# A gated block's first turn: the low halves of W2 move from GpSimd to VectorE, one behind each gate product

## What is computed

```python
x = x + jnp.tanh(g_xattn[0]) * _L0_xattn_ref(ctx_1024, _layernorm(x, axis=-1), ...)
x = x + jnp.tanh(g_ffn[0]) * _L0_ffn_ref(_layernorm(x, axis=-1), ...)

def _expert_ffn(x, w1, wg, w2):
    return jax.nn.silu(x @ w1) * (x @ wg) @ w2
# in _L0_ffn_ref:
output = _expert_ffn(x, Ws1, Wsg, Ws2)
for e in range(NUM_ROUTED):                       # 7 experts, the best 3 of each row count
    w_e = jnp.sum(topk_probas * (topk_idxs == e), axis=-1)
    output = output + _expert_ffn(x, W1[e], Wg[e], W2[e]) * w_e[..., None]
```

## Time and profile before

| | |
|---|---|
| median of 3 runs | 1408.97 us (1408.61 to 1411.01) |
| profiled execution | 1408.53 us, span 1406.7 us |
| TensorE matmul busy | 1362.3 us (97%) |
| VectorE busy | 964.6 us (69%) |
| ScalarE busy | 618.5 us (44%) |
| GpSimd busy | 413.5 us (29%) |
| chain that ended last | PE 82%, DVE 11%, issue 4%, ACT 2% |

### The profile page before, as it was taken

The page is one execution under the profiler, slowest core; times in us unless marked ns, Lnnn a source line. Parts: engine busy times, 40 slices in busy tenths (PEclk is TensorE's granted clock), DMA queues, the critical chain, the costliest instruction groups (busy, mean ns, idle before and its releaser), DMA issues.

```text
span 1406.7 us, 18118 instructions
## 1 busy us (share of the span) xinstructions
PE 1362.3 (97%) x6290; PEld 1065.3 (76%) x6290; DVE 964.6 (69%) x1107; ACT 618.5 (44%) x1007; POOL 413.5 (29%) x224
## 2 busy tenths in 40 slices
PE   9888799999999999999999999999999999999999
PEld 4454577777777877888888877888888888888887
DVE  6999856799999764689888765598888732112111
ACT  6887455766556225544543235534543222111111
POOL 0000044788889310123332120133332211111111
PEclk8999999999999999999999999999999999999999
DMA  6344336676667853654565653655665555555552
GB/s 219 108 155 157 135 122 233 253 266 240 227 231 270 284 181 125 199 165 156 187 202 194 256 193 112 205 158 164 196 202 182 200 189 194 194 193 179 179 179 89
DMA packets 90797, 266.38 MB, mean 189 GB/s; under 512 B 11472, under 2 KB 11600, under 8 KB 90336
## 3 DMA queue, kind: packets, MB, share of 16 engines
q1 hardware_dynamic: 85472, 258.39, 53.6%
q10 hardware_dynamic: 5248, 6.96, 1.4%
HBM read 207.39 MB, written 57.93 MB: 189 GB/s over the span
## 4 chain that ended last, share of the span: by engine, by line
PE 82%; DVE 11%; issue 4%; ACT 2%; DMA 0%; ACTq 0%; DVEq 0%; POOL 0%
PE ps_hg L474 24%; PE ps_h L474 21%; PE ps_y L474 16%; PE ps_y L633 8%; DVE st L1180 7%; PE ps_mid L552 6%; DVE y_rows L1186 1%; DVE st L1171 1%; PE ps_mid L522 1%; PE ps_mid L515 1%; PE ps_mid L518 1%; PE ps_mid L474 1%; ACT dA L836 1%; PE ps_h L544 0%; PE ps_y L497 0%
## 5 line engine op out<-in xcount | busy, mean ns | idle before, releaser
L1444 POOL TENSOR_TENSOR h_lo<-h_tmp,h_hi 128x512 fp32r<-128x512 f32 x128 | 256.9, 2007 | 743.9 <-ACT h_hi L913 700.7
L474 PE MATMUL ps_h<-x_hi,w_split 128*128 128x512 f32 x1024 | 345.9, 399 | 1.6 <-DVE x_lo L1239 1.4
L474 PE MATMUL ps_hg<-x_hi,wg_split 128*128 128x512 f32 x1024 | 345.0, 398 | 0.1
L1309 DVE TENSOR_TENSOR h_tmp<-h_tmp,ps_hg 128x512 f32<-128x512 f32 x128 | 88.0, 688 | 318.5 <-PE ps_hg L474 317.5
L1180 DVE TENSOR_TENSOR_SCAN st<-dA,st 128x1024 f32<-128x1024 f32 x128 | 305.8, 2398 | 0.0
L474 PE MATMUL ps_y<-w_split,h_hi 128*128 128x512 f32 x1024 | 258.1, 400 | 0.0
L913 ACT ACTIVATE h_hi<-h_tmp 128x512 fp32r<-128x512 f32 x128 | 80.6, 630 | 350.0 <-DVE h_tmp L1309 350.0
L474 PEld LDWEIGHTS ps_h<-x_hi,w_split 128*128 128x128 f32 x1024 | 192.3, 188 | 42.0 <-DVE x_lo L1239 1.7
L474 PEld LDWEIGHTS ps_hg<-x_hi,wg_split 128*128 128x128 f32 x1024 | 192.3, 188 | 39.8 <-issue 0.5
L474 PEld LDWEIGHTS ps_y<-w_split,h_hi 128*128 128x128 f32 x1024 | 190.3, 190 | 38.5
L907 ACT ACTIVATE h_tmp<-ps_h 128x512 f32<-128x512 f32 x128 | 76.2, 595 | 293.1 <-PE ps_h L474 293.1
(11 more groups left out here) (143 smaller groups left out, 1127.5 us busy)
## 6 DMA issues: line engine op xcount, KB each, us to landing
w_split<-split_scratch SPq DMA_DIRECT2D x192, 512.0 KB, 5.0
wg_split<-split_scratch SPq DMA_DIRECT2D x96, 512.0 KB, 4.2
split_scratch<-w_split SPq DMA_DIRECT2D x64, 512.0 KB, 3.7
b_all<-xd_scratch SPq DMA_DIRECT2D x64, 256.0 KB, 4.1
split_scratch<-wg_split SPq DMA_DIRECT2D x32, 512.0 KB, 3.0
w_raw<-in_W_dram SPq DMA_DIRECT2D x14, 1024.0 KB, 7.1
wg_raw<-in_Wg_dram SPq DMA_DIRECT2D x7, 1024.0 KB, 9.7
dA<-in_x_dram SPq DMA_DIRECT2D x4, 1024.0 KB, 7.8
```

The source lines that it names most:

```text
L474: mm = pe.matmul(out_, lhs[a], rhs[c], start=first and q == 0, stop=last and q == len(sides) - 1)
L1309: dve.tensor_tensor(h_tmp[j % 2][:], h_tmp[j % 2][:], ps_hg[:], ALU.mult).then_inc(h_made, 1)
L1444: pool.tensor_tensor(h_lo[:, j, :], h_tmp[j % 2][:], h_hi[:, j, :].bitcast(F32), ALU.subtract).then_inc(hl_ready, 1)
```

## The change

In steps 1 to 7 of the first turn VectorE makes the low half of tile j of W2 directly behind product j. GpSimd's row of four is gone. TensorE, ScalarE and SyncE keep their instructions and their order.

```diff
+            def down_low(step, j):
+
+                dve.wait_ge(w2h, T * step + j + 1)
+                dve.tensor_tensor(half(2, j, 1), w_raw[2][:, j], half(2, j, 0).bitcast(F32), ALU.subtract).then_inc(w2l, 1)
+
             def step_(step, e, between=lambda p: None):
+
+                splits = isinstance(step, int) and 0 < step < STEPS
...
                     dve.tensor_tensor(h_tmp[j % 2][:], h_tmp[j % 2][:], ps_hg[:], ALU.mult).then_inc(h_made, 1)
+                    if splits:
+                        down_low(step, j)
                     between(2 * j + 1)
...
-            def split_down(step, tiles=range(T)):
-                for j in tiles:
-                    pool.wait_ge(w2h, T * step + j + 1)
-                    pool.tensor_tensor(half(2, j, 1), w_raw[2][:, j], half(2, j, 0).bitcast(F32),
-                                       ALU.subtract).then_inc(w2l, 1)
...
-                if split:
-                    split_down(step + 1)
```

## The result

The changed kernel takes 1480.67 us (median of 4 runs, 1479.36 to 1481.9) against 1408.79 us for the kernel before on the same chip (4 runs, 1407.59 to 1411.01): a ratio of 1.0508 [1.0493, 1.0523], 71.9 us slower. The profiled execution took 1481.8 us, with a span of 1480.0 us against 1406.7. The prediction said 1471 us, range 1440 to 1495.

A forecast was written before the change was run, and what follows sets the result against it. TensorE and VectorE both nearly full in a 41.06 us step, stretches hanging on VectorE's order. Step 2 17.4, four periods 42.6, step 7 1.2, clock 1.5: 62.7 us on 1408.5 gives 1471 us, range 1440 to 1495.

The forecast's parts named there:

- the queue: SyncE's DMAs behind the late W2 flag: 13.0 us from first issue to the row's landing, bounds 11 and 15.
- the clock: TensorE slow after resting at g = 10 in the down phase: 0.3 us for each of five rests, 1.5 us.
- four periods: Between the five late rows of steps 2 to 6: 51.7 us each against 41.06, together 42.6 us more.
- step 7: No row to wait for, two subtractions ahead of the residual: 1.2 us.
- the forecast of 271.3: Step 2: raw W1 lands at 271.3, not 260.5, behind 6.8 MB taking 19.8 us; ScalarE wants it at 263.14.
- the working of step 2: Late raw W1, then the late row, put product 0 of step 3 at 323.9, not 306.54: 17.4 us later.
- the prediction's walk: One step summed stretch by stretch from row landing to row landing: 51.7 us, with 14.2 from landing to product 0.
- The subtractions: Four added on VectorE per step, 0.60 us each: 2.4 us a step if port waits stay as they are.
- rival 1: Row comes in time after all, only VectorE's 2.4 us a step count: 14 us, 1423 us; chance 0.10.
- rival 2: GpSimd off the shared port makes VectorE faster, a step gains 1.9 us: 9.5 us, 1399 us; chance 0.04.
- Rival 3: Raw loads late in every step, not step 2 alone, each of four periods 3 us longer: 1483 us; chance 0.10.
- where PE waits for nothing: Place of GpSimd's removed row, 7.74 us a step: gives back GpSimd's time and perhaps some of VectorE's through the port.

The follow-up runs named there:

- Experiments 1: Kernel before, late flag alone: each W2 store on SyncE also waits for its product, GpSimd's row kept, no VectorE subtraction; 1465.51 us, ratio 1.0394.
- experiment 4: Changed kernel with SyncE's DMAs interleaved: W2 store j ahead of tile j's up stores, row behind tile 1's, raw W2 last; 1417.82 us, ratio 1.0053.
- experiment 2: Kernel before, GpSimd's row and early flag kept, plus an unused VectorE subtraction behind each product of steps 1 to 7; 1427.75 us, ratio 1.0134.
- experiment 3: Changed kernel with the load of the row of slots 8 to 11 issued before the W2 stores in steps 2 to 6; 1458.84 us, ratio 1.0347.
- Experiments 7: Kernel before with GpSimd's four W2 subtractions replaced by one-column memsets raising the same flags, low halves left stale; 1405.24 us, ratio 0.9972.
- experiment 9: Changed kernel with all four VectorE subtractions ahead of product 0, SyncE's order as in the kernel before; 1404.72 us, ratio 0.997.
- experiment 8: Changed kernel with interleaved SyncE order and VectorE's subtractions in pairs ahead of products 0 and 2; 1412.69 us, ratio 1.0029.

## Why the prediction came out as it did

**The mechanism was right.** VectorE waits for a DMA once in each of steps 2 to 6, ahead of the row product of slot 8; TensorE waits behind it; ScalarE waits once for raw W1; later steps are untouched. Experiments 1 and 4 show that flag and queue are the cause: one makes the loss without VectorE's work, the other has VectorE's work without the loss. The sum was 62.7 us and 73.3 were measured on the profiled execution's span. The missing 10.6 us are two terms sized too small, the queue (8.5 us) and the clock (5.5), and two sized too large (0.7 us in each of four periods, 0.8 in step 7); the rest comes to 0.2 us. That the sum is no further off is in part luck, as the errors have opposite signs.

**The queue: 13.0 us, measured 14.4.** From the first DMA behind the flag to the row's landing the five steps took 13.45, 16.0, 14.4, 13.4 and 14.8 us. I had argued that 13.0 should do because the queue starts empty, where the one that it was copied from had three stores ahead. The rate was lower: 315 GB/s in the window above against 344. Over the four periods the mean is 14.65, so 1.65 us each, 6.6 us. In step 2 the same queue makes ScalarE's wait end at 274.34:

```profile
274.34 0.63 ACT L898 ACTIVATE w_split<-w_raw 128x512 fp32r<-128x512 f32 x1 [9.56 <-DMA w_raw<-in_W_dram]
```

That row is from ACT's timeline of the changed kernel; the forecast of 271.3 was 272.9 with the 1.6 us by which this execution was late already, so 1.4 us more. The first row landed another 0.5 us late.

**The clock: 1.5 us for all rests, measured 7.0.** Two rows of PE's timeline, changed kernel:

```profile
287.42 1.11 PE L552 MATMUL ps_mid<-ident,st 128*128 128x128 f32 x4 [10.43 <-DVE st L1180]
...
318.23 1.09 PE L552 MATMUL ps_mid<-ident,st 128*128 128x128 f32 x4 [7.15 <-DVE y_rows L1186]
```

Four transposes take 1.1 us here and 0.66 at full clock. In step 2 TensorE rested from 277.0 to 287.4; the granted clock was 0.50 (1.2 GHz) from 282.2 on and stayed there until 292.4, 5.0 us into the work. Product 2 came 5.8 us after these transposes instead of 3.5: 2.3 us, which the working of step 2 had at nothing. Behind the five landings the work ran at 0.50 for 4.9, 4.9, 3.1, 4.7 and 5.9 us. Half of it is lost, 1.5 to 3.0 us each time, where I had taken 1.7 at most from the earlier trace rows. Of these 1.6 us were in hand by the prediction's walk, and from landing to product 0 it took 14.9, 14.9, 14.3, 14.8 and 15.3 us instead of 14.2: 3.1 us more in all, least where the low clock was shortest and most where it was longest. In the chain that stretch is now TensorE's from 318.23 on without a gap, where I had VectorE as the one waited for. A seventh stretch stands in step 5, from 449.4 to 452.8, behind a rest of 1.86 us at g = 4; steps 3, 4 and 6 have the same rest and keep a clock of 1.00. There product 2 comes 10.1 us behind product 1 and not 8.5: 1.6 us more, 7.0 in all. The Trainium skill ("TensorE: Matmul & The Clock Gate", section "HAM oscillation — how this bites in real kernels") says that rests which come back in a loop make each following piece start slow; the prediction had 8.5 us by that and set it aside for 1.5. The trace agrees with the rule that there is a slow start behind every one of the six long rests. As to the price, the five behind the landings, for which the two sums were made, cost 3.1 us: between my 1.5 and the 8.5. That these 3.1 us are the clock's is read from the chain and from how they follow its length; no run has the waits without the low clock.

**The subtractions: 2.4 us a period, right with the queue, too much without it.** Between "late flag only" and the changed kernel the period differs by 2.4 us (51.2, 53.6), as the sum had it. Without the queue it was 1.07 (experiment 4), which makes rival 1 (the row in time) worth 8.5 us where the prediction said 14. The 1.07 are what is left of two things of opposite sign: VectorE's work costs 3.4 us a period with GpSimd's row beside it (experiment 2), 1.6 of them by the clock, and 2.3 are gone without the row, 1.6 of them again the clock. In the 2.4 the clock has a part as well: between product 0 of step 3 and of step 7 TensorE works 21.9 us at 0.50 in the changed kernel and 15.2 in "late flag only", of which half, 3.3 us or 0.8 a period, is lost at most. Groups of the changed kernel (busy us, mean ns of one | idle before):

```profile
L1180 DVE TENSOR_TENSOR_SCAN st<-dA,st 128x1024 f32<-128x1024 f32 x128 | 297.6, 2335 | 0.0
L1171 DVE TENSOR_TENSOR st<-u,b_all 128x1024 f32<-128x1024 f32 x128 | 177.0, 1393 | 54.4 <-DMA b_all<-xd_scratch 52.8 <-PE ps_mid L552 1.4
L1296 DVE TENSOR_TENSOR w_split<-w_raw,w_split 128x512 fp32r<-128x512 f32 x28 | 24.9, 891 | 0.0
```

Scans and row products were busy 305.8 and 182.9 us before: together 14.1 us of port waits are gone, and the 28 subtractions cost 24.9, at a mean of 0.89 us. So rival 2 had a true mechanism and too small a size. In the changed kernel's walk it shows behind product 0: from there to the transposes of g = 4 it took 11.4 us, not 12.1. The prediction had put the subtraction behind product 0 on the path, but product 1 stands 6.4 us behind product 0, as before.

**Steps 7 and 2.** Step 7 cost 0.4 us, not 1.2. Step 2 cost 22.2 us, not 17.4: 1.4 the queue ahead of W1, 2.3 the clock, 0.5 the queue ahead of the row, 0.7 the stretch behind it.

**Rival 3** (raw loads late in every step) did not come with this change: ScalarE waited for raw weights once. The prediction's remark that W1 lands just when it is wanted was right, though, and experiment 3 shows it: with the row out of the queue the wait is there in every step, 7.4 us each.

**One claim about the place was only half right.** The prediction put the row of four "where PE waits for nothing" and so gave its removal no price. Experiments 7 and 9 show that it was worth 0.82 us a period, 4 us in all, if the work that replaces it stays at the beginning of the step.

Two things stay open. Why the queue's length varies between 13.4 and 16.0 us from step to step was not tried. And of the 2.4 against 1.07 us for the same subtractions, with the queue and without, the clock explains 0.8 us at most; the rest is measured but not taken apart.

## What to carry to other kernels

Before moving the producer of a flag, list everything that the issuing queue has written behind each wait on it, with the bytes, and ask when each of these is wanted; the loss here was not in the 28 operations moved but in 3.9 MB of transfers that left together, some 20 us later, and pulling the first late one forward only uncovered the next. Ask of an operation that is twice as fast on the other engine where it stands there and when its flag comes: here the same four subtractions gave 72 us of loss behind the products (8.5 with the order of the DMAs mended) and no loss, but a gain of 2.9 to 4.5 us, ahead of them.
- A VectorE subtraction of 128x512 takes 0.68 us where nothing is in its way, 0.91 to 1.48 us in 14 of the 28 of the changed kernel, and 3.47 us for two in the pair that alternates with GpSimd's. Of GpSimd's own the shortest is 1.29 and the longest 4.22: that one starts while VectorE has the row times u, waits out VectorE's four, and ends 1.2 us behind them. The Trainium skill ("SBUF — State Buffer", section "Who interferes with whom") has it that a VectorE operation with two SBUF inputs and a GpSimd one that reads SBUF contend for one port pair, which is locked by one of them at a time. The trace agrees. Who comes next is not always the same: in experiment 8 the two engines alternate, in experiment 9 four of VectorE's pass ahead of one of GpSimd's.
- A DMA of 0.25 MB took 9.5 us from issue to landing behind a full queue and 3.8 us without one, and raw W1, 1 MB, 16.16 us in experiment 3 against 6.1: the duration of a DMA says what is ahead of it, not what it is.
